# Last 8 edge tiles summed into nodes on TensorE instead of by GpSimd's adding scatters

## The reference, cut to what matters

```python
xn = _layernorm(x)
# graph part: mean of the edge features per node, then two dense layers
sums = segment_sum(edge_attr, src, num_segments=n)
counts = segment_sum(ones, src, num_segments=n)
edge_attr_agg = sums / max(counts, 1.0)[:, None]
gnn = relu(concat([xn, edge_attr_agg, u[batch]]) @ W1 + b1) @ W2 + b2
x = x + gnn + mix(xn)          # mix: linear attention of 8 heads, second order features
x = x + moe(_layernorm(x))     # 8 experts, the two best per node
```

## Time and profile before

| | us |
|---|---|
| median of three runs (1161.19 to 1167.14) | 1162.53 |
| profiled execution | 1170.63 |
| its span in the trace | 1168.9 |
| POOL busy | 783.9 |
| PE busy | 929.1 |
| DVE busy | 666.4 |
| ACT busy | 372.0 |

### The profile page before, as it was taken

The page is one execution under the profiler, slowest core; times in us unless marked ns, Lnnn a source line. Parts: engine busy times, 40 slices in busy tenths (PEclk is TensorE's granted clock), DMA queues, the critical chain, the costliest instruction groups (busy, mean ns, idle before and its releaser), DMA issues.

```text
span 1168.9 us, 21027 instructions
## 1 busy us (share of the span) xinstructions
PE 929.1 (79%) x6782; PEld 683.5 (58%) x6783; DVE 666.4 (57%) x1997; ACT 372.0 (32%) x984; POOL 783.9 (67%) x568
## 2 busy tenths in 40 slices
PE   4899798798799999989989999840898632999950
PEld 2445343343478878878768788730786631777740
DVE  4689777587766666656646565301574553333324
ACT  3333423221234434433333334310353321333310
POOL 5688888888888888888888888886003358333330
PEclk8699898898899999999989999975797865999985
DMA  9876545545365565555565554437623313333349
GB/s 317 205 146 113 77 76 77 77 67 86 23 111 88 84 104 86 96 86 94 87 95 86 95 86 41 41 31 171 196 68 101 89 64 115 97 105 97 103 111 263
DMA packets 151952, 121.39 MB, mean 104 GB/s; under 512 B 121361, under 2 KB 141205, under 8 KB 148024
## 3 DMA queue, kind: packets, MB, share of 16 engines
q0 software_dynamic: 64992, 29.93, 24.9%
q1 hardware_dynamic: 81726, 78.00, 23.6%
q10 hardware_dynamic: 5146, 12.33, 3.4%
HBM read 75.23 MB, written 46.03 MB: 104 GB/s over the span
## 4 chain that ended last, share of the span: by engine, by line
POOL 48%; issue 16%; PE 15%; DMA 14%; DVE 3%; SPq 1%; ACT 1%; another core or an unknown queue 1%; ACTq 0%; POOLq 0%; DVEq 0%
POOL edge_sums L672 46%; DMA edge_sums<-sums,addr 9%; PE ps L1270 4%; PE ps L1254 4%; PE ps L1194 2%; DMA r2t<-expert_outputs 2%; PE ps L1248 2%; POOL routed_rows L691 1%; DMA edges<-in_edge_attr 1%; PE ps L1255 1%; PE ps L1184 1%; DMA edges<-edge_sums 1%; SPq L566 1%; SPq L567 1%
## 5 line engine op out<-in xcount | busy, mean ns | idle before, releaser
L672 POOL DMA_INDIRECT edge_sums<-sums,addr x416 | 648.1, 1558 | 145.2 <-issue 120.1
L834 ACT ACTIVATE r<-ps 128x500 f32<-128x500 f32 (+1 forms) x225 | 126.4, 586 | 105.8 <-PE ps L1065 75.4
L959 PE MATMUL ps<-edges,same 128*128 128x65 f32 x832 | 116.3, 284 | 24.3 <-DVE same L1322 16.8
L959 PEld LDWEIGHTS ps<-edges,same 128*128 128x128 f32 x832 | 103.7, 196 | 47.1 <-issue 34.2
L731 ACT ACTIVATE sums<-ps 128x260 f32<-128x260 f32 x104 | 40.5, 392 | 273.1 <-DMA edge_sums<-sums,addr 155.2
L1322 DVE SCALAR_TENSOR_TENSOR same<-srow,src_f,below 128x128 f32<-128x128 int32 x416 | 118.3, 346 | 5.6 <-DMA srow<-in_src_row 5.6
L1065 PE MATMUL ps<-ident,r2t 125*128 125x125 f32 x800 | 109.8, 281 | 13.3 <-ACT r L839 10.4
L1432 DVE TENSOR_TENSOR r2t<-ps,r 125x2048 f32<-125x2048 f32 x50 | 113.2, 2263 | 0.0
L703 POOL DMA_INDIRECT expert_outputs<-r x56 | 55.0, 982 | 83.7 <-DVE r L1690 69.2
L1093 PE MATMUL ps<-r 128*64 128x125 f32 x1600 | 108.7, 278 | 0.0
L999 PE MATMUL ps<-r2t,r 125*64 125x512 f32 x400 | 107.0, 672 | 1.1 <-issue 1.1
(11 more groups left out here) (232 smaller groups left out, 1389.5 us busy)
## 6 DMA issues: line engine op xcount, KB each, us to landing
srow<-in_src_row SPq DMA_DIRECT2D x26, 1024.0 KB
edges<-in_edge_attr SPq DMA_DIRECT2D x26, 512.0 KB
r<-routed_rows SPq DMA_DIRECT2D x56, 129.0 KB
edge_sums<-sums,addr POOLq DMA_INDIRECT x416
hpre_rows<-r ACTq DMA_DIRECT2D x25, 250.0 KB
r<-hpre_rows SPq DMA_DIRECT2D x25, 250.0 KB
edge_sums<-r SPq DMA_DIRECT2D x4, 1040.0 KB, 14.1
r2t<-in_ew SPq DMA_DIRECT2D x4, 1024.0 KB, 12.8
```

Of the source, the lines that this page charges most:

```text
L672: pool.indirect_dma_start(out=tables[k], out_offset=bass.IndirectOffsetOnAxis(ap=addr[:, j:j + 1], axis=0), in_=sums[:, j % OR, :], in_off ...
L834: act.activation(phT[0:rows, j // 2 % 2 * 2 + j % 2, :], bank(1 + j % 2, rows, 0, QC * P), ACT.Copy).then_inc(grp_ready[j % 2], 1)
L959: m = mm(bank(b, 128, c0 + k * F, c0 + (k + 1) * F), lhsT=same[:, j % SR, :], rhs=edges[:, h, j % CH, :], start=True, stop=True)
```

## The change

The last eight tiles (`HT`; groups 102 and 103) are no longer compared, de-duplicated, copied and scattered. `ETS` = 408 tiles and `NGR` = 102 groups remain for that. The eight go another way:

- DVE, ahead of tile 24 of pass 2 (`place_late`), makes two one-hot matrices for each late tile from the node numbers. A node is number 25 p + t: `where_p` (128 edges x 125) marks p, `where_t` (128 edges x 25) marks t.
- ACT, after the last `x1`, copies the rows of the eight edge tiles into PSUM (banks 4 and 6) and signals `edges_kept`.
- DVE multiplies them out, one late tile at a time, to `spread` (128 edges x 25 x 65, two buffers): row times `where_t`.
- PE multiplies `where_p` with `spread` in four matmuls of 455, 455, 455 and 260 columns into banks 0 to 3, and adds up over the eight tiles.
- DVE adds the tables as before, table 1 between the seventh and the eighth late tile, tables 2 and 3 behind the eighth, and then adds the four banks.

POOL makes the row of numbers that the one-hots are compared with (`node_lo`) by an iota at group 1, in place of zeros that are needed only at the start. Tables 1 and 3 are read back to other buffers (`edges`, `sums`), table 1 behind `edges_kept`. The last row load of the comparisons has half its size. One semaphore (`ssq_ready`) becomes a `link`, a count on DVE's own semaphore.

```diff
@@ -21,7 +21,9 @@
     G4 = 4
-    NGR = ET // G4
+    HT = 8
+    ETS = ET - HT
+    NGR = ETS // G4
     TW = 80
@@ -52,7 +54,8 @@
     SC2, SC4 = SC * SC, SC ** 4
-    assert T == 25 and NGR == 104 and G4 * (EA + 1) <= BANK - 250
+    BT = 7
+    assert T == 25 and ET == 416 and ETS % CH + HT == CH and HT <= 2 * BT and G4 * (EA + 1) <= BANK - 250
@@ -73,12 +76,18 @@
         spare_row = sb("spare_row", [128, 1])
+        where_t = sb("where_t", [128, HT, T])
         srow = sb("srow", [128, 2, CH * 128], i32)
...
         sums = sb("sums", [128, OR, TW])
+        late_src = src_off[:, ETS:ET]
+        late_slot = rank[:, ETS:ET]
+        late_room = srow[:, (NCH - 1) % 2, (CH - HT) * 128:].bitcast(fp32)
+        where_p = late_room[:, 0:HT * P].rearrange("p (h n) -> p h n", h=HT)
         below = sb("below", [128, 128])
         zeros = sb("zeros", [128, 128])
+        node_lo = zeros[:, 0:P]
         ones = sb("ones", [128, 128])
...
@@ -179,6 +188,7 @@
         cmax = carve([P, T])
+        spread = carve([128, 2, T, F], at=r1_off[0])
         hs = carve([128, 2, MC * P])
...
@@ -396,8 +406,8 @@
-            w = (srow[:, 0, :].bitcast(fp32), srow[:, 1, :].bitcast(fp32), same[:, :, :].rearrange("p r c -> p (r c)"),
-                 edges[:, :, :, :].rearrange("p h c f -> p (h c f)"))[k]
+            w = (srow[:, 0, :].bitcast(fp32), edges[:, :, :, :].rearrange("p h c f -> p (h c f)"),
+                 same[:, :, :].rearrange("p r c -> p (r c)"), sums[:, :, :].rearrange("p r f -> p (r f)"))[k]
             return w[0:P, 0:T * TW].rearrange("p (t f) -> p t f", t=T)
@@ -476,8 +486,9 @@
                 wait(sp, same_ready, CH * (c - 1))
-                sp.dma_start(srow[:, c % 2, :], src_row[c * CH:(c + 1) * CH, :].rearrange("c p -> (c p)")
-                             .rearrange("(a n) -> a n", a=1).to_broadcast([128, CH * 128])).then_inc(srow_loaded[c % 2], 16)
+                n_ = min(CH, ETS - c * CH)
+                sp.dma_start(srow[:, c % 2, 0:n_ * 128], src_row[c * CH:c * CH + n_, :].rearrange("c p -> (c p)")
+                             .rearrange("(a n) -> a n", a=1).to_broadcast([128, n_ * 128])).then_inc(srow_loaded[c % 2], 16)
@@ -528,10 +539,12 @@
-            sp.wait_ge(same_ready, ET)
+            sp.wait_ge(same_ready, ETS)
             sp.wait_ge(dedup_ps, NGR)
...
                 sp.wait_ge(added[k], 16 * NGR)
+                if k == 1:
+                    sp.wait_ge(edges_kept, 1)
                 for a, z in PARTS:
@@ -664,6 +677,8 @@
                 pool.wait_ge(sums_ready, g + 1)
+                if g == 1:
+                    iota(node_lo, [[T, P]])
                 for k in range(G4):
@@ -855,6 +870,13 @@
+
+            act.wait_ge(x1_ready, T)
+            act.wait_ge(edges_loaded[(NCH - 1) % 2], 16 * ((NCH - 1) // 2 + 1))
+            for b, (h0, h1) in ((4, (0, BT)), (6, (BT, HT))):
+                z = act.activation(bank(b, 128, 0, (h1 - h0) * F),
+                                   edges[:, (NCH - 1) % 2, ETS % CH + h0:ETS % CH + h1, :].rearrange("p c f -> p (c f)"), ACT.Copy)
+            z.then_inc(edges_kept, 1)
@@ -1167,6 +1189,13 @@
             pe.wait_ge(x1_ready, T)
+            for h in range(HT):
+                pe.wait_ge(same_ready, ETS + h + 1)
+                for q, a in enumerate(range(0, T, BT)):
+                    z = min(a + BT, T)
+                    m = mm(bank(q, P, 0, (z - a) * F), lhsT=where_p[:, h, :], rhs=spread[:, h % 2, a:z, :].rearrange("p t f -> p (t f)"),
+                           start=(h == 0), stop=(h == HT - 1))
+                m.then_inc(dedup_ps, 1)
             pe.wait_ge(mean_ready, 1)
@@ -1321,9 +1350,9 @@
                                            below[:, :], ALU.is_equal, ALU.mult, accum_out=rank[:, j:j + 1]).then_inc(same_ready, 1)
-                if (g + 1) * G4 % CH == 0:
-                    here = slice(c * CH, (c + 1) * CH)
-                    v.wait_ge(same_ready, (c + 1) * CH)
+                if (g + 1) * G4 % CH == 0 or g == NGR - 1:
+                    here = slice(c * CH, (g + 1) * G4)
+                    v.wait_ge(same_ready, (g + 1) * G4)
                     link(v.scalar_tensor_tensor(rank[:, here], rank[:, here], 1.0, src_off[:, here], ALU.is_equal, ALU.mult))
@@ -1362,8 +1391,7 @@
                 wait(v, ksq_ready, t + 1)
-                v.tensor_reduce(ssq[:, u, :], phi[:, u, :, 0, :], AX.X, ALU.add).then_inc(ssq_ready, 1)
-                wait(v, ssq_ready, t + 1)
+                link(v.tensor_reduce(ssq[:, u, :], phi[:, u, :, 0, :], AX.X, ALU.add))
                 link(v.tensor_scalar(nm[:, u, :], ssq[:, u, :], EPS2, 1.0 / SC2, ALU.max, ALU.mult))
@@ -1504,14 +1532,51 @@
-            tiles(pass2, 2)
+            def place_late():
+
+                late = src_f[:, ETS:ET]
+                v.wait_ge(consts, 20)
+                link(v.tensor_scalar(late_src[:, :], late, T - 1.0, None, ALU.subtract))
+                for h in range(HT):
+                    z = v.scalar_tensor_tensor(where_p[:, h, :], node_lo, src_f[:, ETS + h:ETS + h + 1], ones[:, 0:P],
+                                               ALU.is_le, ALU.mult, accum_out=late_slot[:, h:h + 1])
+                link(z)
+                for h in range(HT):
+                    z = v.scalar_tensor_tensor(where_p[:, h, :], node_lo, late_src[:, h:h + 1], where_p[:, h, :],
+                                               ALU.is_ge, ALU.mult)
+                link(z)
+                link(v.scalar_tensor_tensor(late_slot[:, :], late_slot[:, :], -float(T), late, ALU.mult, ALU.add))
+                link(v.tensor_scalar(late_slot[:, :], late_slot[:, :], float(T), float(T), ALU.add, ALU.mult))
+                for h in range(HT):
+                    z = v.tensor_scalar(where_t[:, h, :], node_lo[:, 0:T], late_slot[:, h:h + 1], None, ALU.is_equal)
+                link(z)
+            tiles(pass2, 2, ((T - 1, place_late),))
...
             acc = table_sb(0)
-            v.wait_ge(tables_back[0], 32)
-            for k in range(1, G4):
+
+            def add_table(k):
+
                 v.wait_ge(tables_back[k], 32)
                 link(v.tensor_tensor(acc[:, :, 0:F], acc[:, :, 0:F], table_sb(k)[:, :, 0:F], ALU.add))
+
+            v.wait_ge(edges_kept, 1)
+            for h in range(HT):
+                b, c0 = (4, h * F) if h < BT else (6, (h - BT) * F)
+                if h > 1:
+                    v.wait_ge(dedup_ps, NGR + h - 1)
+                v.tensor_tensor(spread[:, h % 2, :, :], bank(b, 128, c0, c0 + F).unsqueeze(1).to_broadcast([128, T, F]),
+                                where_t[:, h, :].unsqueeze(2).to_broadcast([128, T, F]), ALU.mult).then_inc(same_ready, 1)
+                if h == HT - 2:
+                    v.wait_ge(tables_back[0], 32)
+                    add_table(1)
+            for k in range(2, G4):
+                add_table(k)
+            v.wait_ge(dedup_ps, NGR + HT)
+            for q, a in enumerate(range(0, T, BT)):
+                z = min(a + BT, T)
+                link(v.tensor_tensor(acc[:, a:z, 0:F], bank(q, P, 0, (z - a) * F).rearrange("p (t f) -> p t f", t=z - a),
+                                     acc[:, a:z, 0:F], ALU.add))
             link(v.tensor_scalar(cmax, acc[:, :, EA], 1.0, None, ALU.max))
```

6 lines of the change are left out of this document (3 added, 3 removed).

## The result

The changed kernel takes **1144.76 us** (median of 4 runs, 1143.37 to 1147.9) against 1163.47 us for the kernel before on the same chip (4 runs). The ratio is 0.984, interval 0.981 to 0.987: 18.7 us less.

The account below looks back on a forecast made before the run. Bound by POOL's scatter stream with a bare tail: eight scatters fewer give 14.86 us, four PSUM adds cost 2.4, products hide, so 12.4 us off the 1162.53 median gives 1150.1 us, range 1146.5 to 1156.5.

Parts of the forecast that it names:

- The tail is bare and the table reads end last: End of aggregation: nothing covers the last scatters and table reads, so shortening them by 14.86 us counts in full.
- Pass 2 moves with the stream: Attention pass: held back by scatters, it ends 14.8 us earlier, last x1 at 759.3; other bound, unmoved at 774.15.
- the gate still decides: Pass 2: ACT's last copy still waits for a landed scatter, opened at 737.0, against 736.4 less some work without gates.
- Products end last: Rival at the join: pass 2 unmoved and all eight products at the lower clock; 5.3 us slower, 1167.8; chance 0.04.
- half of the tail stays: Rival at the join: traffic, not issue, sets last scatter's landing and last read; gain about 6 us, 1156.5; chance 0.06.
- slowed scatters: Rival on POOL: place_late's DVE work lengthens the scatters beside it by 1.0 us; gain 11.4, 1151.1; chance 0.03.
- the eighth product decides: Rival at the join: the eighth late product outlasts its 0.8 us of cover; gain about 10.5 us, 1152; chance 0.12.
- What is removed: Scatter stream on POOL: eight scatters fewer, so the last starts at 785.69 instead of 800.55, 14.86 us earlier.
- Small edits: POOL's iota, SP's new wait, halved row load, link, tables' other homes: nothing, at most 0.3 us for the iota.
- What follows keeps its order: Stretch after the divisor: unchanged, starting at the low clock before and after, so the 12.4 us gain carries through.
- Part is given back after the join: Rival behind the join: two or three more low-clock spells leave a gain of about 8 us, 1154.5; chance 0.12.
- All of it and a luckier clock: Most favourable rival, whole kernel: the full gain plus better clock spells, 15 us, 1147.5; chance 0.05.

Follow-up runs that it names:

- no_late: The changed kernel with everything for the late tiles left out (one-hots, copy, products, PSUM adds, iota), so eight edge tiles are missing: 1147.57 us, ratio to before 0.985.
- eighth_first: The changed kernel with DVE's eighth multiplication ahead of all table adds: 1143.88 us, ratio to before 0.982.
- after_again: The changed kernel, unaltered, timed and profiled a second time: 1145.70 us, ratio to before 0.984.
- before_iota: The kernel before with only POOL's iota at group 1 added, into a buffer nobody reads by then: 1161.23 us, ratio to before 0.999.
- late4: The changed kernel with four late tiles instead of eight (HT = 4): 1157.49 us, ratio to before 0.994.

## Where the prediction held, and the terms that failed

What held, by its steps:

- *The tail is bare and the table reads end last.* Eight scatters less brought 15.0 us in no_late (13.3 to 16.4, by which trace of before it is held against), forecast 14.86.
- *Pass 2 moves with the stream.* The last x1 ended at 754.30, forecast 759.3. But "the gate still decides" doesn't hold for all of pass 2: tiles 6 to 22 now take 17.70 us each, as long as tiles that no scatter holds up (17.80 in the old trace), and twelve late tiles don't move it any further. It didn't matter for the join.
- *place_late is hidden and takes 6.7 us.* It ran from 725.19 to 731.85, 6.7 us; DVE then still idled 2.51 us before the copy ahead of x1 of tile 22, where it had idled 8.68 (and 9.07 in no_late). The prediction counted twelve small operations, there are eleven; the sum came out all the same. The three scatters beside it took 1.55, 1.59 and 1.55 us. The Trainium skill (SBUF — State Buffer, SBUF: two separate sides) says that DVE in a two-port mode keeps GpSimd from writing descriptors. By the prediction's reckoning that would have been 2.4 us; this trace doesn't bear it out, with 0.04 us at most (1.59 us beside 1.55).
- *The products.* Forecast 5.7 us at the lower clock and 3.0 at the higher: the eighth took 5.78, the middle ones 2.73 (starts of their multiplications on DVE). The eighth was done before table 3's add *ended*, as forecast. TensorE paced DVE, which waited 0.88 or 0.89 us for it four times in a row.
- *Four PSUM adds.* Forecast 2.4 us, measured 2.43.
- *The rivals.* "Products end last", "half of the tail stays" and "slowed scatters" are refuted by the rows above; "the eighth product decides" by the 2.69 us that the add ahead of the join waited for table 3, and by eighth_first.

The time lies below the range because two terms of the sum were mis-sized, both in the same direction:

- *The place of the last scatter ("What is removed", with the "Small edits" at nothing).* Forecast 785.69, measured 780.80 and 779.34. The prediction took one trace's stream, cut eight scatters off its end, and took everything ahead of them as given. From the twentieth scatter to the last, the old trace has 396 intervals in 740.0 us, 1.869 each, the new one 388 in 721.9, 1.860 each. That is 3.2 us, of which 6 ns on each scatter make 2.3: those go with the iota, which the prediction priced at "nothing, at most a small operation's 0.3 us". The other 1.6 us is the twentieth scatter itself (58.95 against 60.55). The landing and read behind the last scatter took 0.7 us more than before, so the join came 4.1 us before its forecast of 807.3, and 5.3 us in after_again.
- *The rest after the join ("What follows keeps its order").* The prediction took it unchanged, 349.1 us. About 4 us of that was the stretched SP queue, and belongs to the profiled execution alone. The changed kernel's 338.4 and 339.1 are 6 to 8 us below the 345.1 to 346.3 of the traces of before that had no other change after the join. The prediction had this place as a rival, "Part is given back after the join", with the note that the spells "may as well fall better", and they did. Its most favourable case, "All of it and a luckier clock", was 15 us, less than the 18.7 measured.

Together these are the 14.9 us by which the span fell below the forecast 1156.5. By medians the miss is only 5.3 us (1144.76 against 1150.1), and the earlier join alone (4.1 and 5.3 us) is about that. How the miss of the medians divides between the two can't be told finer: the rest is known from one or two executions of each kernel, the traces of the changed kernel lie 1.4 and 2.8 us below their medians and those of before and the kernels made from it from 0.8 us below to 7 us above theirs, and before_iota shows that the iota's part alone isn't measurable. late4, whose gain fits the sum, says that most of the excess doesn't come from the small edits. Why eight tiles have 6.6 us more than the sum, twelve 3.5 and four 1.5 stays open, with intervals of 3 to 4 us on each.

## What to carry to other kernels

A bare stream of equal instructions on one engine is worth its pitch times the number removed. But where the last one stands varies from execution to execution (here by 3 us in six traces), so that the 0.2 us between 14.86 and 15.0 was in part luck. Before a profile's stage is taken as fixed, profile the kernel a second time and look in the first trace for issues that take twice their usual time (here eight in 17.2 us). The shares of the chain of waits vary as well: 46% and 38% for one line of one kernel. Where TensorE resumes behind stalls, give the range a few microseconds on both sides: stages of the same 1447 instructions took 338 to 349 us, for the larger part by how much of them ran at the lower clock. And before an instruction is said to act on those behind it, look at those ahead of it.

## What the runs showed of the hardware

- In the seven traces of programs with one more iota on POOL (128x125, 0.83 us, at about 25 us) the adding scatters had a median of 1548 or 1549 ns, in the seven without it 1553 or 1554. A memset in its place didn't do it, and one behind it didn't undo it. The difference is there from the first scatter on (1675 or 1676 against 1680 to 1682 ns at about 18 us), ahead of the iota, so it belongs to the program and not to what the iota does when it runs. How is open.
- In the stage after the join TensorE waited 7.2 to 9.7 us for the input of a layer-2 batch, 26 times in the fourteen traces. The batch of eight instructions behind the pause always took 3.47 to 3.78 us; the one after it took 1.89 us 17 times and 3.62 us nine times. One such batch more at the lower clock is 1.7 us, and it came and went between traces.
- Counted by the granted clock, the same work of TensorE came out within 1% in all fourteen traces (223 to 225 us), while its busy time was 235 to 244 us.
- The last adding scatter (128 rows of 80 numbers) was seen landed 7.7 to 9.8 us after its start in the fourteen traces.
- In one of fourteen traces eight DMA issues on SP took 17.22 us instead of 8.2.
